# A last stage run inside the last expert: finishing all tokens beside its matmuls and patching the expert's own rows

## What is computed

```python
x1  = x + cross_attention(layernorm(x))                  # kept for the end
y   = layernorm(x1)
src = rmsnorm(y + gqa(y), norm1_w)
# routing: top 2 of 8 experts by sigmoid(src @ gate_w), weights normalised,
# at most 1280 rows an expert, in token order; rows over that are dropped
h   = gelu(padded_rows[e] @ w1[e])                       # (1280, 1024)
out = h @ w2[e]                                          # (1280, 512)
src = src + sum of weight * out over the token's experts
result = x1 + rmsnorm(src, norm2_w)                      # rsqrt(mean(src^2) + 1e-6)
```

## Time and profile before

| | us |
|---|---|
| median of 3 runs | 3271.99 |
| lowest, highest | 3271.33, 3275.97 |
| span of the profiled execution | 3274.8 |
| last expert's last eviction starts | 3214.05 |
| busy: PE, DVE, POOL, ACT | 3105.0, 2092.2, 2025.4, 1606.1 |

### The profile page before, as it was taken

How to read it: one execution, slowest core, us unless ns; L and a number is a source line. 1 busy time by engine, 2 the same in 40 slices (tenths; PEclk the granted TensorE clock), 3 DMA queues, 4 the chain that set the end, 5 groups by cost and what they waited for, 6 DMA issues and landing times. The chain is left out here.

```text
span 3274.8 us, 45482 instructions
## 1 busy us (share of the span) xinstructions
PE 3105.0 (95%) x16824; PEld 2006.0 (61%) x16824; DVE 2092.2 (64%) x3805; ACT 1606.1 (49%) x3249; POOL 2025.4 (62%) x880
## 2 busy tenths in 40 slices
PE   6998999999999999999999999985999999999992
PEld 5775444544544544544545545424999899889992
DVE  6887787788788788787887887813333333333334
ACT  3441565656656566565665655652333334334332
POOL 2442799899899899899899998982111111111114
PEclk9997899999999999999999999996999999999996
DMA  4664522001011022201101001022333333333237
GB/s 129 212 210 150 154 113 99 11 24 50 21 33 43 18 62 56 50 17 44 33 21 48 24 28 41 14 82 77 73 91 72 99 73 80 84 74 94 49 78 269
DMA packets 135519, 245.49 MB, mean 75 GB/s; under 512 B 30263, under 2 KB 35383, under 8 KB 132773
## 3 DMA queue, kind: packets, MB, share of 16 engines
q1 hardware_dynamic: 117232, 206.56, 19.6%
q0 software_dynamic: 16640, 35.42, 6.2%
q10 hardware_dynamic: 1461, 1.11, 0.1%
HBM read 127.82 MB, written 117.57 MB: 75 GB/s over the span
## 5 line engine op out<-in xcount | busy, mean ns | idle before, releaser
L1256 DVE TENSOR_REDUCE home_mxp<-p_ps_a 128x1 f32<-128x512 f32 x2021 | 1253.4, 679 | 267.9 <-PE p_ps_a L1455 265.5
L1175 ACT ACTIVATE p_PR<-p_ps_b 128x512 f32<-128x512 f32 x2048 | 1061.3, 605 | 646.3 <-PE p_ps_b L1469 633.1
L1036 POOL TENSOR_TENSOR p_PP<-p_PP,p_PR 128x2048 f32<-128x2048 f32 x223 | 1023.3, 4589 | 57.0 <-ACT p_PR L1175 35.9
L1455 PE MATMUL p_ps_a<-home_K,home_Q 96*128 96x512 f32 x2021 | 805.7, 429 | 8.1 <-PEq L58 4.8
L1469 PE MATMUL p_ps_b<-home_Q,home_K 98*128 98x512 f32 x2048 | 787.8, 425 | 7.0 <-ACT p_PR L1175 6.8
L1745 POOL DMA_INDIRECT src_d<-p_YE,p_token x80 | 123.5, 1543 | 828.8 <-DVE p_YE L1871 765.2
L1032 POOL TENSOR_TENSOR p_PP<-p_PR 128x2048 f32<-128x2048 f32 x127 | 583.4, 4594 | 79.3 <-ACT p_PR L1175 75.3
L1455 PEld LDWEIGHTS p_ps_a<-home_K,home_Q 96*128 96x128 f32 x2021 | 380.9, 192 | 331.3 <-DVE home_mxp L1256 213.0
L1469 PEld LDWEIGHTS p_ps_b<-home_Q,home_K 98*128 98x128 f32 x2048 | 384.7, 189 | 309.0 <-ACT p_PR L1175 239.0
L1479 PE MATMUL p_ps_pv<-p_PR,p_VS 128*32 128x512 f32 x4096 | 514.6, 603 | 0.0
L1790 ACT ACTIVATE p_hf<-p_ps_h 128x384 f32<-128x384 f32 (+1 forms) x256 | 112.0, 438 | 575.9 <-PE p_ps_h L85 572.1
(11 more groups left out here) (194 smaller groups left out, 3239.0 us busy)
## 6 DMA issues: line engine op xcount, KB each, us to landing
weights_w_raw<-in_L_ffn_w SPq DMA_DIRECT2D x16, 2048.0 KB, 8.5
xe_d<-p_SR SPq DMA_DIRECT2D x20, 1056.0 KB, 9.9
home_Q<-qh_d SPq DMA_DIRECT2D x64, 256.0 KB, 3.8
p_XE<-xe_d SPq DMA_DIRECT2D x16, 792.0 KB, 4.6
src_d<-p_SR SPq DMA_DIRECT2D x9, 1024.0 KB, 6.3
p_XE<-xe_d SPq DMA_DIRECT2D x16, 528.0 KB, 3.6
p_X<-in_x SPq DMA_DIRECT2D x8, 1024.0 KB, 7.9
x_d<-p_x SPq DMA_DIRECT2D x8, 1024.0 KB, 5.3
```

What stands on the lines that cost most here:

```text
L1036: nc.gpsimd.tensor_tensor(PP[:, buf, :, :], PP[:, buf, :, :], PR[:, tile_at(u, tile), :, :], ALU.add).then_inc(add_made, 1)
L1175: nc.scalar.activation(PR[:, tile_at(u, kt), j, :], ps_b[:, n % BK, :], ACT.Exp, scale=SCALE).then_inc(ex_made, 1)
L1256: nc.vector.reduce_max(mxp[:, a // (S // CH), a % (S // CH):a % (S // CH) + 1], ps_a[:, bank, :], AXX).then_inc(a_read, 1)
L1455: nc.tensor.matmul(ps_a[:, bank, :], QS[u % QK][0:96, j, t * P:(t + 1) * P], KS[u % KV][0:96, kb * CH:(kb + 1) * CH], start=True, stop=Tru ...
```

## The change

- `src` and `x1` lie side by side in one DRAM tensor `pairs` (a row is `src` then `x1`, 4 KB); it has the 512 spare rows, of which the `x1` half is now zeroed too. Token numbers are doubled for the scatter-adds of experts 0 to 6, since the adds index half rows.
- `phase_combine` is gone, and with it the loads of `src` and `x1` for it.
- In the last expert, after all adds of experts 0 to 6 have landed, all 4096 tokens are finished as if they were not in expert 7: 16 "duos" of 256 tokens. SP loads a duo (1 MB) into one of four buffers in the room of the raw weights, ACT squares its two tiles, POOL makes the powers and multiplies the odd tile by `norm2`, DVE multiplies the even one, and then (`duo_done`, one duo later) scales both and adds `x1`; SP stores 512 KB to the output. Each duo has a place in every engine's program: `DUO_UP` behind steps of up blocks, `DUO_EARLY` and `DUO_DOWN` around rows.
- The rows of expert 7 itself: POOL gathers the pairs of a tile's tokens (`fetch`, 512 KB); DVE adds weight times product (`row_made`), ACT squares, POOL makes the power, DVE scales and adds `x1` (`row_done`); POOL scatters the finished rows over the output (`put`, with a bounds check that skips the spare tokens), not before all duos are stored. Puts 0 to 5 stand ahead of row 6's power.
- PE does down(6, 3) ahead of up(7, 0); a tile's product waits for `row_made` two tiles before it.
- The last expert's `w2` is split in block 0, not in block 1.

The diff, cut to what is said above:

```diff
 def phase_attend(...)
+            sp.dma_start(x1_pad.rearrange("(t p) d -> p t d", p=P), SR[:, 0, :, 0:D]).then_inc(zero_st, 16)
...
 def phase_experts(...)
+    LAST = E - 1
+    HEAD = NT * LAST
+    DUO_UP = {(0, 7): 0, (1, 1): 1, (1, 3): 2, (1, 5): 3, (1, 7): 4, (2, 2): 9, (2, 5): 10, (3, 2): 15}
+    DUO_EARLY = {0: 5, 3: 11}
+    DUO_DOWN = {0: 6, 1: 7, 2: 8, 3: 12, 4: 13, 5: 14}
+    FLUSH = (3, 5)
+    LR, GR, RR, RS = 4, 2, 6, 3
+    ROW, DUO = 3, 3
+    PUT_BEFORE = {6: (0, 1, 2, 3, 4, 5), 8: (6,), 9: (7,)}
...
     # SP
+            def load_duo(i):
+                if i >= LR:
+                    hold(sp, lin_st[i % LR], 16 * (i // LR))
+                sp.dma_start(plain[i % LR], pairs[2 * P * i:2 * P * (i + 1), :]...).then_inc(lin_in[i % LR], 16)
+            def store_duo(i):
+                hold(sp, lin_step, DUO * i + DUO)
+                sp.dma_start(out_rows[2 * P * i:2 * P * (i + 1), :]..., plain[i % LR][:, :, 0, :]).then_inc(lin_st[i % LR], 16)
...
+            sp.wait_ge(w1l_made, DK * E)
+            rows_added(sp, HEAD)
+            for i in range(2):
+                load_duo(i)
...
+            load_block(LAST, 3)
             hold(sp, w2l_made, FK * E)
-            for c in range(NC):
-                if c == NC // 2:
-                    hold(sp, h_mm, FK * NB * E)
-                sp.dma_start(kept.x1(c), x1_d[c].rearrange("(t p) d -> p t d", p=P)).then_inc(kept.x1_in[2 * c // NC], 16)
-            rows_added(sp, E * NT)
-            load_rows(sp)
+            for i in range(2, LR):
+                load_duo(i)
+            for i in range(DUOS):
+                store_duo(i)
+                if 0 < i <= DUOS - LR:
+                    load_duo(i - 1 + LR)
+            all_plain_stored(sp)
+            for n in range(NT - RS, NT):
+                row_stored(sp, n)
     # POOL
+            def fetch(n):
+                if n >= GR:
+                    pool.wait_ge(row_step, ROW * (n - GR) + ROW)
+                nc.gpsimd.indirect_dma_start(out=pair_at[n % GR]..., in_=pairs, in_offset=...token...).then_inc(got_in[n % GR], 16)
+            def put(n):
+                if n == 0:
+                    all_plain_stored(pool)
+                hold(pool, row_step, ROW * n + ROW)
+                nc.gpsimd.indirect_dma_start(out=out_rows, out_offset=...token..., in_=done[:, n % RR, :],
+                                             bounds_check=N - 1, oob_is_err=False).then_inc(row_st[n % RS], 16)
+            def duo(i):
+                power_plain(i)
+                odd_plain(i)
...
+            rows_added(pool, HEAD)
+            for n in range(GR):
+                fetch(n)
+            for b in range(NB):
+                for f in range(FK):
+                    if (b, f) in DUO_UP:
+                        duo(DUO_UP[b, f])
+                if b > 0:
+                    for n in range(FIRST[b - 1], FIRST[b]):
+                        if n in DUO_EARLY:
+                            duo(DUO_EARLY[n])
+                        for m in PUT_BEFORE.get(n, ()):
+                            put(m)
+                        power_row(n)
+                        if n in DUO_DOWN:
+                            duo(DUO_DOWN[n])
+                        if n + GR < NT:
+                            fetch(n + GR)
+            for n in range(FIRST[NB - 1], NT):
+                for m in PUT_BEFORE.get(n, ()):
+                    put(m)
+                power_row(n)
+            for n in range(max(PUT_BEFORE[NT - 1]) + 1, NT):
+                put(n)
     # DVE
+            def duo_done(i):
+                dve.wait_ge(lin_rs, i + 1)
+                dve.wait_ge(lin_step, DUO * i + 1)
+                dve.wait_ge(lin_odd, i + 1)
+                for k in (2 * i, 2 * i + 1):
+                    nc.vector.scalar_tensor_tensor(plain_rows(k)[:, 0, :], plain_rows(k)[:, 0, :], rstd[:, k:k + 1], plain_rows(k)[:, 1, :],
+                                                   ALU.mult, ALU.add).then_inc(lin_step, 1)
+            def duo(i):
+                if i > 0:
+                    duo_done(i - 1)
+                even_plain(i)
+            def row_made(b, n):
+                dve.wait_ge(y_mm, HEAD + n + 1)
+                dve.wait_ge(got_in[n % GR], 16 * (n // GR) + 16)
+                nc.vector.scalar_tensor_tensor(pair[:, 0, :], ps_y[:, n % 2, :], weight..., pair[:, 0, :], ALU.mult, ALU.add).then_inc(row_step, 1)
+                if n >= RR:
+                    row_stored(dve, n - RS)
+                nc.vector.tensor_tensor(done[:, n % RR, :], pair[:, 0, :], norm_row[:], ALU.mult).then_inc(row_step, 1)
+            def last_rows(b):
+                for n in range(FIRST[b], FIRST[b] + TILES[b]):
+                    if n in DUO_EARLY:
+                        duo(DUO_EARLY[n])
+                    row_made(b, n)
+                    if n in DUO_DOWN:
+                        duo(DUO_DOWN[n])
+                    row_done(n)
     # PE
+                    if final and n >= 2:
+                        pe.wait_ge(row_step, ROW * (n - 2) + 1)
+            def last_body():
+                down(LAST - 1, NB - 1)
+                for b in range(NB):
+                    up(LAST, b, False, b == NB - 1)
+                    if b > 0:
+                        down(LAST, b - 1, False, True)
+                down(LAST, NB - 1, False, True)
...
-def phase_combine(nc, kept, norm_row, SR, sr_in, out):
...
 def build_layer(...)
-    x1_d, y_d = (scratch(n, (NC, CH, D)) for n in ("x1_d", "y_d"))
-    src_rows = scratch("src_d", (N + CH, D))
+    pairs = scratch("pairs_d", (N + CH, 2 * D))
+    src_d, x1_d = (pairs[:, D * i:D * (i + 1)].rearrange("(n q) d -> n q d", q=CH) for i in range(2))
```

More of the change, by code:

```diff
@@ L1722, in _ @@
[L1722 to L1732 removed]
+            sp.wait_ge(meta_made, META * (NB * LAST + 1))
@@ new lines, in put @@
+            def put(n):
+                b = max(b for b in range(NB) if FIRST[b] <= n)
+                if n == 0:
+                    all_plain_stored(pool)
+                hold(pool, row_step, ROW * n + ROW)
+                nc.gpsimd.indirect_dma_start(out=out_rows, out_offset=bass.IndirectOffsetOnAxis(ap=token[:, b, n - FIRST[b]:n - FIRST[b] + 1].bitcast(U32), axis=0),
+                                             in_=done[:, n % RR, :], in_offset=None, bounds_check=N - 1, oob_is_err=False).then_inc(row_st[n % RS], 16)
@@ L1749, in _ @@
+            nc.gpsimd.memset(half[:], -0.5).then_inc(ident_made, 1)
+            for e in range(LAST):
                 for b in range(NB):
@@ L1779, in rows_high, with hidden @@
                     nc.scalar.activation(xTh[:, b % 2, k, 0:n], ps_t[:, k % 2, 0:n], ACT.Copy).then_inc(xh_made, 1)
-            def hidden(e, b, first=False, with_w2=False, last=False):
+            def hidden(e, b, first=False, with_w2=False, last=False, duos={}):
                 n = TILES[b] * P
@@ L1798, in hidden, with square_plain @@
                         split_w2(e, W2_SPLIT[f])
+                    if (b, f) in duos:
+                        duo(duos[b, f])
             def before_block(e, b):
                 return NT * e + FIRST[b - 1] if b >= 1 else NT * e - TILES[NB - 1]
-            def body(e, first=False, last=False):
+            def square_plain(k):
+                act.wait_ge(lin_in[k // 2 % LR], 16 * (k // 2 // LR) + 16)
+                if k > 0:
+                    act.wait_ge(lin_ss, k)
+                if k < 2 * DUO_UP[1, 7]:
+                    unread = done[:, RR - 1, :]
+                else:
+                    act.wait_ge(x_tr, DK * (NB * E - 1))
+                    unread = XE[:, 0, 0, 0:D]
+                nc.scalar.activation(unread, plain_rows(k)[:, 0, :], ACT.Square, accum_out=ss[:, k:k + 1]).then_inc(lin_ss, 1)
@@ new lines, in row_done @@
+            def row_done(n):
+                pair = pair_at[n % GR]
+                dve.wait_ge(row_rs, n + 1)
+                dve.wait_ge(row_step, ROW * n + 2)
+                nc.vector.scalar_tensor_tensor(done[:, n % RR, :], done[:, n % RR, :], rstd_e[:, n:n + 1], pair[:, 1, :], ALU.mult, ALU.add).then_inc(row_step, 1)
+            def last_rows(b):
+                for n in range(FIRST[b], FIRST[b] + TILES[b]):
+                    if n in DUO_EARLY:
+                        duo(DUO_EARLY[n])
+                    row_made(b, n)
+                    if n in DUO_DOWN:
+                        duo(DUO_DOWN[n])
+                    row_done(n)
@@ L1885, in _ @@
             body(0, first=True)
-            for e in range(1, E - 1):
+            for e in range(1, LAST):
                 body(e)
-            body(E - 1, last=True)
-            rows_out(E - 1, NB - 1)
+            last_body()
         @block.tensor
@@ L1919, in up, with down @@
                         transposes(e + (b + 1) // NB, (b + 1) % NB, BETWEEN[f])
-            def down(e, b, first=False):
+            def down(e, b, first=False, final=False):
                 m = NB * e + b
@@ L1946, in _ @@
             body(0, first=True)
```

(7 more changed lines are left out.)

254 lines of the change are left out of this document (140 added, 114 removed).

## The result

The changed kernel takes 3236.39 us in the median of four executions (3234.72 to 3238.44), the kernel before 3271.66 (3270.78 to 3275.97): a ratio of 0.9885 with an interval of 0.9873 to 0.9897, or 35.3 us less. The forecast was 3228, 43.8 us less; the result lies in its range of 3220 to 3246, 8 us above the forecast.

The account below looks back on a forecast made before the run. PE bounds the kernel up to 3214.0 us, then a 60.8 us tail; 3214.0 + stall 8 + remaining end 9 = 3231.0 against 3274.8, 43.8 less, so 3228.2 from the median 3271.99; range 3220 to 3246.

Parts of the forecast that it names:

- What goes: End of the kernel: all 60.8 us of tail behind the last matmul, with the combine phase's loads, arithmetic and last store, disappear.
- S: PE's stall in the last expert, mainly behind rows 0 to 2: 8 us, ends 3 and 14.
- POOL's multiply holds DVE ... 10 us of DVE delay ... the stall grows to 7: Last expert: 16 POOL multiplies delay DVE instructions reading two SBUF operands, 10 us in all; stall behind rows 0 to 2 becomes 7.
- Rival A: Last expert: POOL's powers hold DVE as well, 17 us of DVE waiting, stall 20 to 23, time 3240 to 3246; chance 0.2.
- A walk gives a stall of 3 to 4 if every engine keeps its durations: Rows 0 to 2: stepping through the semaphores with four duos and three rows at present durations stalls PE 3 to 4 us.
- The clock term: Last expert: loss from PE's clock falling in a stall, taken as zero.
- D: Duo loads: gathers and stores on the same engines stretch them to 10 to 14 us, time 3242 to 3262; chance 0.05.
- C: Duo loads 4 to 15: the four-buffer ring sets the pace, kernel slower, break-even at 16 us loads, median 3278; chance 0.03.
- B: Last expert: all added work is hidden beside PE, stall 0 to 2 us, time 3220 to 3222; chance 0.12.
- Put(9) lands 2.8, the end 1 later: Kernel's end: the last row scatter lands 2.8 us after its start and the span ends 1 us after that.
- 0 to 2 more behind puts 0 to 5: Last expert: 0 to 2 us more PE stall because these puts stand ahead of row 6's power on POOL.
- L: What stays behind PE's last product until the end: 8.5 us, high end 11.5, taken as 9.

Follow-up runs that it names:

- the run with the written order: Changed kernel with own finished tiles for rows 6 to 9 and, at POOL's end, powers and gathers ahead of puts that can wait; its span ends at 3235.4 us.

## Why the prediction was right or wrong

- **What goes, and faster at all: right.** Nothing of the 60.8 us was left, and PE's own work costs the same in the new order (M 116.9 in the run without the four duos against 115.8 before).
- **Where PE stalls: right.** Rows 0 to 2, seen as 4.45 and 1.66 us in block 2's `up`, released by ACT's `hf` and DVE's `xTl`. It nowhere waits at the last product. S 9.4 for 8. In the sum this is near; it is partly luck, as the next bullets show: its terms were wrong in opposite directions.
- **"POOL's multiply holds DVE ... 10 us of DVE delay ... the stall grows to 7": the mechanism right, its size wrong.** This is the step that failed behind a nearly right sum. A DVE instruction with two operands in SBUF that begins inside a multiply of POOL does end only behind it, as I read from the earlier trace rows. But I let all 16 multiplies hold DVE for half their length, and only 7 DVE instructions were held, for 3.9 us in all instead of 10: DVE waits for POOL's multiply by program before it finishes a duo, so none of the duo and row instructions with two operands in SBUF began inside one but in its last 0.01 us. PE gains 1 to 3 us where the multiplies are gone, and not the 4 that I had added to the walk. The Trainium skill's rule (GPSIMD Engine Reference, Key points), that GpSimd contends with DVE instructions with two SBUF inputs, is borne out here for POOL's multiply of two tensors and not for its powers.
- **Rival A, powers hold DVE too (0.2): fell.** `hl` runs at 421 and 557 ns with all 26 powers in place. The pair in the earlier trace rows could not have told: those scalings read one tensor from SBUF, not two. The other direction exists: POOL's powers are stretched beside DVE, from 0.715 and 0.559 to 1.02 and 0.92 in the median:

```profile
L1846 POOL TENSOR_TENSOR p_rstd<-p_sv,p_half x16: 690/1024/1078, 3119.4 to 3198.4; 128x2 f32<-128x2 f32 x16
L1859 POOL TENSOR_TENSOR p_rstd_e<-p_sv_e,p_half x10: 554/916/965, 3146.0 to 3227.9; 128x1 f32<-128x1 f32 x10
```

- **"A walk gives a stall of 3 to 4 if every engine keeps its durations": too small.** The walk had POOL's row at 5.1 to 5.6 us and fitted, and no term for a gather landing 6.6 us after an issue that itself stands behind a duo. No run here separates these terms well enough to say how they share out the rest of the waits (6.1 us, of which the second, 1.66, is likely POOL's multiply).
- **The clock term at zero: wrong, 2 to 3 us.** I named it as what would prove me wrong; it is a quarter to a third of S.
- **Loads of 6 to 8 us: nearly right** (7.6 at the median, 9.4 at most). D (10 to 14 us) and C (a load of 16) fell, though their sign showed once: one of six waits of ACT's squares for a load was 4.6 us. B (all hidden) fell.
- **"Put(9) lands 2.8, the end 1 later": mis-sized by 2.4 us.** Between put(9)'s start and the end lie 6.2 us (6.3 in the run with the written order). The put lands after 2.1, 0.7 earlier than I had it, and the end is 4.1 behind that instead of 1: I took the 1 from a kernel whose last work is a store, and here the end waits for POOL's drain behind an indirect DMA.
- **"0 to 2 more behind puts 0 to 5": the right place, booked on the wrong side.** PE never waited; DVE waited 7.83 us at row 6 for put(3), and 2.5 us of that reached the last eviction through gathers 8 and 9. I had the wait for a finished tile nowhere in L. In the second profile of the same kernel little of it arrives (T 11.8), so 2 us of the 4.3 are this execution's own.

Sum: S + 1.4, put and end + 2.4, late eviction + 2.5, the way to put(9) - 0.1, and the 0.5 that the forecast had rounded up in L - 0.5: 5.7 us.

The measured 3236.4 is just inside the forecast's own range (3222.7 to 3236.7); the rest of the range, up to 3246, was there for rival A, which fell. The sign that I had set for the end, 8.5 to 11.5 us from the last product's eviction, came true with 10.8, since the eviction itself was late by 2.5.

## What to carry to other kernels

When a whole stage is laid beside a busy engine, cost the crowded stretch as a walk in which every step has its own landing time, and look for waits that are within a microsecond or two of each other: removing the one that the trace names may give nothing, because the next takes its place. Leaving out the work itself, not the waits, shows what the stretch costs. A term for one engine holding another needs a count of how often they can meet in the written order, and not only a price for each meeting. An engine that stalls for 4 us can lose half as much again at a lower clock afterwards, as PE did here (4.45 us of wait, 2 to 3 us behind it). And look at what the last engine's program ends with: here 4.1 us lie behind the last landing.
